# First graph layer of a four-part network: scores issued three pairs ahead with four exp buffers, adjacency transposes through one PSUM bank

## What is computed

```python
y = jnp.linalg.norm(x, axis=-1, keepdims=True)
A = x @ x.T / (y @ y.T) * b
A = jnp.tanh(A / 8.0) * 8.0
A = jnp.exp(A) * A_shape                      # A_shape is the adjacency matrix
A = A / jnp.sum(A, axis=-1, keepdims=True)
x = A @ x
return x @ W.T + bias
```

## Time and profile before

| | |
|---|---|
| median of 3 runs | 1024.88 us (1022.98 to 1025.22) |
| profiled execution, its own time | 1025.94 us |
| its span | 1024.3 us |
| mean granted TensorE clock | 0.842 |
| TensorE matmuls busy in the span | 719.9 us (70%) |
| VectorE | 666.3 us (65%) |
| ScalarE | 451.5 us (44%) |
| first part: first scores / last row sums start | 17.05 us / 159.74 us |

### The profile page before, as it was taken

One profiled execution on the slowest core, in us unless ns is written; L12 is line 12 of the kernel. 1 busy time (PEld: TensorE's weight loads), 2 busy tenths in 40 slices (PEclk: granted clock), 3 DMA queues, 4 the chain that ended last, 5 costly groups with the idle time before them and its releaser, 6 DMA issues.

```text
span 1024.3 us, 14187 instructions
## 1 busy us (share of the span) xinstructions
PE 719.9 (70%) x4705; PEld 529.0 (52%) x4705; DVE 666.3 (65%) x2073; ACT 451.5 (44%) x612; POOL 208.5 (20%) x476
## 2 busy tenths in 40 slices
PE   3999996715999205689999987326855955676274
PEld 2455454314988203358877856115635743666144
DVE  6555656501333227787766516999999999995958
ACT  3877771002333002443445338538656855811041
POOL 3400000274221475000000002213134134310000
PEclk9999996756999656889999999658778877888678
DMA  9176000123777210000000000000000000201001
GB/s 187 29 121 204 1 1 1 52 77 96 218 214 206 71 52 20 1 1 1 2 2 1 2 1 2 0 0 2 1 1 2 2 1 1 83 1 28 0 1 42
DMA packets 49704, 44.12 MB, mean 43 GB/s; under 512 B 7136, under 2 KB 46432, under 8 KB 49120
## 3 DMA queue, kind: packets, MB, share of 16 engines
q1 hardware_dynamic: 37600, 26.47, 8.8%
q0 software_dynamic: 12032, 16.78, 8.0%
HBM read 40.09 MB, written 11.53 MB: 50 GB/s over the span
## 4 chain that ended last, share of the span: by engine, by line
DVE 32%; PE 23%; ACT 3%; issue 3%; DVEq 1%; SPq 0%; DMA 0%; ACTq 0%
PE bank L1763 6%; PE bank L1709 6%; PE bank L1722 4%; DVE big L1296 4%; DVE cand L1227 3%; DVE rm L1128 3%; PE bank L1746 3%; DVE hacc L1222 3%; DVE big L1287 2%; DVE big L1284 2%; DVE cand L1245 2%; DVE top L1240 1%; ACT big L1577 1%; ACT big L1550 1%; PE bank L1903 1%
## 5 line engine op out<-in xcount | busy, mean ns | idle before, releaser
L1577 ACT ACTIVATE big<-bank 128x512 f32<-128x512 f32 x128 | 70.4, 595 | 94.3 <-PE bank L1746 94.0
L1709 PE MATMUL bank<-kk,qq 64*128 64x512 f32 x256 | 82.7, 775 | 32.7 <-ACT big L1550 32.7
L1746 PE MATMUL bank<-ident,big 128*128 128x128 f32 x512 | 80.7, 306 | 34.7 <-DVEq L1319 27.6
L1746 PEld LDWEIGHTS bank<-ident,big 128*128 128x128 f32 x512 | 62.3, 155 | 61.0 <-DVEq L1319 28.3
L714 DVE TENSOR_TENSOR big<-big,bank 128x512 f32<-128x512 f32 x32 | 22.0, 688 | 109.1 <-ACT big L756 109.1
L1550 ACT ACTIVATE big<-bank,negm 128x2048 f32<-128x2048 f32 x32 | 62.7, 1960 | 68.6 <-DVE fsc L1323 50.9
L1296 DVE SCALAR_TENSOR_TENSOR big<-big,st 128x2048 f32<-128x2048 f32 x32 | 73.9, 2348 | 14.3 <-PE bank L1746 14.3
L1026 POOL TENSOR_SCALAR bt<-bt 128x1 f32<-128x1 f32 x16 | 3.1, 195 | 364.1 <-ACT big L1567 224.6
L308 DVE TENSOR_TENSOR big<-big,adjT 128x1024 f32<-128x1024 f32 x32 | 40.0, 1251 | 54.9 <-ACT big L362 54.8
L411 PE MATMUL bank<-xnT 128*128 128x512 f32 x128 | 64.1, 624 | 4.5 <-ACT xnT L339 4.0
L829 PE MATMUL bank<-big 128*128 128x256 f32 x256 | 64.1, 395 | 1.0 <-DMA big<-in_L_ffn_w_dram 0.3
(11 more groups left out here) (325 smaller groups left out, 1556.8 us busy)
## 6 DMA issues: line engine op xcount, KB each, us to landing
big<-in_L_ffn_w_dram SPq DMA_DIRECT2D x96, 128.0 KB
big<-in_adj_dram POOLq DMA_DIRECT2D x8, 512.0 KB, 10.1
xs_scratch<-hacc SPq DMA_DIRECT2D x4, 1024.0 KB, 7.0
big<-xs_scratch POOLq DMA_DIRECT2D x32, 128.0 KB, 3.1
ys_scratch<-big SPq DMA_DIRECT2D x32, 128.0 KB, 2.8
kk<-in_adj_dram POOLq DMA_DIRECT2D x4, 512.0 KB, 12.2
qq<-in_adj_dram POOLq DMA_DIRECT2D x4, 512.0 KB, 12.8
res<-in_x_dram SPq DMA_DIRECT2D x4, 256.0 KB, 5.9
```

Source lines behind the costliest of these rows:

```text
L1577: nc.scalar.activation(MT[:, 4 * q:4 * q + 4, s * P:(s + 1) * P], bank[:, 5 + q % 2, :].rearrange("p (j i) -> p j i", j=4), ACT.Copy).then ...
L1709: nc.tensor.matmul(bank[:, c, :], qq[lo:lo + DA, (g * G + s) * P:(g * G + s + 1) * P], kk[lo:lo + DA, c * CH:(c + 1) * CH], start=True, st ...
L1746: mm = nc.tensor.transpose(bank[:, 5 + q % 2, j * P:(j + 1) * P], mk[:, s, jt * P:(jt + 1) * P], ident[:, :])
```

## The change

- The exp output `e2` has EB = 4 buffers in place of two, and exp(q) waits for multiply(q-4) in place of multiply(q-2).
- TensorE issues the scores AHEAD = 3 pairs ahead. In step q of the loop it issues scores(q+3), transposes(q+2), gather(q); it was transposes(q+2), scores(q+2), gather(q). The first scores and turns before the loop are reordered to match.
- All adjacency transposes go through bank 6, so transposes(q) wait for the copy of q-1 in place of q-2.
- ScalarE copies the transposes of q+1 after exp(q), in place of those of q+2. In the start it takes chunk 2's and 3's turned rows, and the normalised tiles, one pair earlier.
- Two waits go that kept bank 7 free for the row sums.

```diff
+        EB = 4
+        AHEAD = 3
...
-            4 * CH * TPC // 2, 2 * PR, 2 * PR, 4 * PR, PR, CH, D, D)
+            4 * CH * TPC // 2, 2 * PR, EB * PR, 4 * PR, PR, CH, D, D)
...
-                    nc.scalar.activation(pair_of(q % NP, q // NP), two(bankb[:, 6 + q % 2, :]), ACT.Copy
+                    nc.scalar.activation(pair_of(q % NP, q // NP), two(bankb[:, 6, :]), ACT.Copy
...
-                    if q >= 2:
-                        act.wait_ge(pm_ready, q - 1)
-                    nc.scalar.activation(e2[:, q % 2, :], e1[:, q % 2, :], ACT.Exp, scale=8.0).then_inc(exp_done, 1)
-                    if q == 0:
-                        take_adjT(1)
-                    if q in (1, 2):
-                        take_wnT(q + 1)
-                    if q in (1, 2, 3):
-                        xn_of(range(q * TPC, (q + 1) * TPC), 2)
-                    if q + 2 < NQ:
-                        take_adjT(q + 2)
+                    if q >= EB:
+                        act.wait_ge(pm_ready, q - EB + 1)
+                    nc.scalar.activation(e2[:, q % EB, :], e1[:, q % 2, :], ACT.Exp, scale=8.0).then_inc(exp_done, 1)
+                    if q in (0, 1):
+                        take_wnT(q + 2)
+                    if q in (0, 1, 2):
+                        xn_of(range((q + 1) * TPC, (q + 2) * TPC), 2)
+                    if q + 1 < NQ:
+                        take_adjT(q + 1)
...
-                    if q >= 2:
-                        pe.wait_ge(tr_out, q - 1)
+                    if q:
+                        pe.wait_ge(tr_out, q)
...
-                            mm = nc.tensor.transpose(bankb[:, 6 + q % 2, (k * TPC + s) * P:(k * TPC + s + 1) * P],
+                            mm = nc.tensor.transpose(bankb[:, 6, (k * TPC + s) * P:(k * TPC + s + 1) * P],
...
-                    pe.wait_ge(tr_out, min((c + 1) * NP + 2, NQ))
...
                 score(0)
+                score(1)
                 turn_adj(1)
-                score(1)
+                turn_wn(1)
+                score(2)
+                turn_wn(2)
                 for q in range(NQ):
                     c, p = divmod(q, NP)
-                    if q < NC - 1:
-                        turn_wn(q + 1)
-                    if q == NC - 1:
+                    if q == 0:
+                        turn_wn(3)
+                    if q == 3:
...
-                    if c and p == 1:
-                        pe.wait_ge(sum_read, c)
+                    if q + AHEAD < NQ:
+                        score(q + AHEAD)
                     if q + 2 < NQ:
                         turn_adj(q + 2)
-                        score(q + 2)
                     gather(q)
```

More of the change, by code:

```diff
@@ L163, in build @@
         e1 = e1.rearrange("p (s n) -> p s n", s=2)
-        e2 = e2.rearrange("p (s n) -> p s n", s=2)
+        e2 = e2.rearrange("p (s n) -> p s n", s=EB)
         pm = pm.rearrange("p (s n) -> p s n", s=4)
@@ L307, in _ @@
                         dve.wait_ge(acc_done, (q - 3) // NP * (NP - 1) + max((q - 3) % NP, 0))
-                    nc.vector.tensor_tensor(two(pm[:, q % 4, :]), two(e2[:, q % 2, :]), pair_of(p, c), ALU.mult
+                    nc.vector.tensor_tensor(two(pm[:, q % 4, :]), two(e2[:, q % EB, :]), pair_of(p, c), ALU.mult
                                             ).then_inc(pm_ready, 1)
```

## The result

| | before | after |
|---|---|---|
| median | 1023.93 us (1022.81 to 1025.22, 4 runs) | 1046.89 us (1045.03 to 1047.86, 4 runs) |
| profiled execution, its own time | 1025.94 us | 1046.38 us |
| its span | 1024.3 us | 1044.7 us |
| mean granted TensorE clock | 0.842 | 0.845 |
| first row sums / last row sums / next part starts | 63.18 / 159.74 / 165.69 us | 74.91 / 183.10 / 188.73 us |

The change costs 22.96 us. The ratio is 1.0225, with a 95% interval of 1.0208 to 1.0242.

The account below looks back on a forecast made before the run. TensorE's own work was taken to bound the first layer's middle. Start 3.3, steady part 15.2, chunk ends 1.9 and end 3.0 summed to 23.4 us more, giving 1048.3 us, range 1042 to 1057.

Parts of the forecast that it names:

- the closed round: First layer, each pair: scores(q+2), transposes(q+1), ScalarE's copy(q+1), tanh(q+1), scores(q+3) wait in a loop, 4.63 us against 3.94.
- The middle is bound by TensorE, and only 3.1 us could come back: First layer, 22 to 160 us: TensorE busy 134.88 of 138 us, so better overlap could return at most 3.1 us.
- The round of 4.63 us: One pair's loop: scores 1.82, transposes to copy 0.65, copy to tanh 0.92, tanh to next scores 1.24; bounds 4.5 to 4.75.
- Steady part and chunk ends, +15.2 and +1.9: Scores(9) to scores(31): 22 periods longer by 4.63 - 3.94 us give +15.2; three chunk ends at 0.63 us give +1.9.
- Start, +3.3: Layer's start: reordered turns and ScalarE's tiles delay the first pairs, scores(9) at 59.1 us against 55.75.
- End, +3.0: Layer's end: from the start of scores(31) to the last row sums 12.4 us, against 9.4 before.
- Exp buffers, bank, waits of bank 7, adjacency loads: nothing: First layer: four exp buffers, one transposes' bank, the dropped bank 7 waits and later adjacency loads cost or gain nothing.
- The delay goes through whole: After the layer: a barrier stands behind it, so all 23.4 us of delay reach the total time.
- the signs that I had named: Layer's profile: period 4.6 us, scores waiting 0.5 us each (12 to 18 total), ScalarE 1.6, scores(9) near 59, clock 1.00.
- the clock's: Rival, chance 0.06: gaps drop TensorE's clock in the layer; 1073 us with a quarter of the pairs, 1147 with all.
- The rival of a shorter round (4.3 us): Rival, chance 0.03: in the steady part shorter hand-overs and scores of 1.72 us make a turn 4.3 us, total 1038 us.
- The rival "not slower": Rival, chance 0.02: tanh(q+1) ends before scores(q+3) are due, TensorE never waits, up to 3.1 us come back: 1022 us.

Follow-up runs that it names:

- b_bank_exp4: The kernel before with one bank for the adjacency transposes in place of two and four exp buffers, old orders kept: 1024.64 us.
- a_two_banks: The changed kernel with the adjacency transposes back in banks 6 and 7 by turns, with their two waits: 1047.83 us.
- a_extra: The changed kernel with one more ScalarE operation per pair ahead of tanh, a copy of the identity into an unread tile: 1053.69 us.

## Why the prediction was right

The forecast was 1048.3 us, 23.4 over before; measured are 1046.89, 22.96 over before (whose median is 1023.93 now, 0.95 below the one that I had added to). The mechanism, the closed round, was right. That the sum came out within 0.5 us of the measured difference is in part luck: the start was 1.4 us too short and the steady part with its chunk ends 1.4 us too long, and the two cancel. Step by step:

- **The middle is bound by TensorE, and only 3.1 us could come back.** Held: no kernel here has a chunk under 34.16 us.
- **The round of 4.63 us.** Right in kind, and a little too long: it is 4.55 us. The term that was mis-sized is tanh's start to the scores it releases, 1.24 taken from the earlier trace rows, 1.16 measured in the steady part. The earlier trace rows show the scores of pair 5, which wait for a second semaphore as well (see the last section). The others (1.82, 0.65, 0.92) came out as taken.
- **Steady part and chunk ends, +15.2 and +1.9.** Scores(9) to scores(31) took 170.73 - 60.42 = 110.3 us against 94.6: +15.7 for a forecast of +17.1. The last scores and the last row sums:

```profile
170.73 1.98 PE L411 MATMUL bank<-xnT 128*128 128x512 f32 x4 [0.35 <-ACT big L359]
...
183.10 1.95 PE L436 MATMUL bank<-ones,big 128*128 128x1 f32 x16 [0.48 <-DVE big L277]
```

  Sixteen of the 22 rounds lie outside the chunk ends; at 0.08 us less each they explain 1.3 of the missing 1.4 us. Two pairs at a chunk's end cost 39.80 - 6 x 4.55 = 12.5 us, 3.4 over two rounds; I had 3.3.
- **Start, +3.3.** It was +4.7: scores(9) at 60.42 us against 55.75. Missing in my sum was a slow TensorE, in two places. First, scores(0) and scores(1) together took 5.9 us (16.97 to 22.91) where I had 5.35, because the slow pace lasted into scores(1); everything up to scores(3) is 0.5 us late by it. The doubled durations show this pace (3.78 us against 1.94 for scores(0)), but the granted clock is listed as 1.00 for that stretch, so that it was the clock is inferred. Second, TensorE stood 2.87 us before scores(3), and the granted clock fell to 1.2 GHz from 32.1 to 35.5 us. Scores(3) and the transposes behind them took 1.4 us longer, of which ScalarE's tiles hid a part: scores(4) came 1.1 us later behind scores(3) than by my working. I had the gap in my working and counted what follows it at full clock. Shorter rounds up to scores(9) gave back some 0.3 us.
- **End, +3.0.** 183.10 - 170.73 = 12.4 us, as taken, against 9.4.
- **Exp buffers, bank, waits of bank 7, adjacency loads: nothing.** Shown by b_bank_exp4 and a_two_banks. In the changed kernel no exp waits for a multiply and no transposes of the adjacency for a copy or a load, from 17 to 190 us.
- **The delay goes through whole.** The next part starts 23.04 us later (188.73 against 165.69), where my sum had 23.4 (the projection behind the last row sums is 0.3 us shorter than before). In the two profiled executions the spans differ by 20.4 us only. The experts' part had a short stretch at full clock there that the execution before had not: the 32 matmuls of its gate took 5.25 us instead of 7.01, first before, then after:

```profile
174.32 7.01 PE L772 MATMUL bank<-big,xnT 128*128 128x16 f32 x32 [0.72 <-DVE xnT L539]
```

```profile
197.37 5.25 PE L773 MATMUL bank<-big,xnT 128*128 128x16 f32 x32 [0.87 <-DVE xnT L540]
```

This is 1.8 of the 2.6 us by which the spans fall short; the rest was not looked for. The medians are 22.96 us apart and don't show such a gain, and one profiled execution of each kernel can't say how often it occurs.

Of the signs that I had named, the waits of the scores are there (26, 15.7 us in total, within 12 to 18), though with 0.35 us each and not 0.5, and so are ScalarE's waits (1.43 us each for 1.6) and scores(31) near 171 us. Scores(9) are later than the 59 us named, and the clock was not 1.00 throughout.

Of the rivals, the clock's came true in one place and not as a state of the layer. Two windows of the kernel after, the granted clock again the first of the last three numbers:

```profile
32.00:35.40 3.40, 3.40 (x13) 1.71 (x12) 1.22 (x1) 2.40 (x7) 0.00 (x0) 0.51 0.00 0
36.00:180.00 144.00, 130.35 (x540) 62.22 (x538) 73.00 (x84) 95.04 (x97) 13.43 (x12) 1.00 0.27 59
```

With a gap of 0.35 us in each round of 4.55 us, and three gaps of 1.69 us at the chunk ends, TensorE kept 2.4 GHz throughout; after the one gap of 2.87 us it had 1.2 GHz for 3.4 us. The length of a gap alone does not decide it: in a_extra the clock fell after the gap of 1.89 us at the first chunk's end and did not after the same gap at the other two (1.00 from 116 to 122 us and from 157 to 164 us). The Trainium skill's "TensorE: Matmul & The Clock Gate", section "A second HAM failure mode: psum-queue depth-cycling", has short idling between groups of matmuls as a cause of a swinging clock. By that rule, at the rival's price, the kernel would have gone to 1073 us or beyond; these gaps did not do it. The rival of a shorter round (4.3 us) has the sign of my error right, but four times its size: the round was 0.08 us shorter than mine, not 0.33. The rival "not slower" (tanh over before scores are due) is refuted by every steady round: the scores wait 0.35 us for tanh.

## What to carry to other kernels

Issuing work further ahead does not by itself decouple engines that run in order. Write down, for one period, which instruction each wait stands behind on its own engine, and add up every closed round. The period is the longest of these sums per pair, and the busiest engine's work is only one of them. A wait that costs nothing (28.1 us of ScalarE for transposes) starts to cost when an instruction that another engine needs is put behind it, and swapping two statements on one engine, or moving one copy on the other, opens the round again. Where the middle is bound by one engine's work, a greater distance can win only at the ends, and has to be weighed against what it does to the start.

## What was not expected of the hardware

- The hand-over from tanh to scores becomes 0.09 us shorter after pair 7. In the changed kernel the scores of pairs 3 to 7 wait on two semaphores (`s_free` for the tanh, `wnT_out` for the turned rows), and from pair 8 on they wait on the tanh alone. Tanh's start to scores' start is 1.25 or 1.26 us for pairs 3 to 7 (50.10 to 51.36 for pair 7), 1.17 for pair 8 (54.71 to 55.88), and 1.16 after. That the second wait costs the 0.09 us is argued and not shown: it was not tried by itself.

```profile
50.10 1.11 ACT L359 ACTIVATE big<-bank,bs 128x1024 f32<-128x1024 f32 x1
...
51.36 1.95 PE L411 MATMUL bank<-xnT 128*128 128x512 f32 x4 [0.44 <-ACT big L359]
...
54.71 1.11 ACT L359 ACTIVATE big<-bank,bs 128x1024 f32<-128x1024 f32 x1
...
55.88 1.98 PE L411 MATMUL bank<-xnT 128*128 128x512 f32 x4 [0.35 <-ACT big L359]
```

- A ScalarE copy of 128 x 128 with a listed 0.30 us takes a slot of 0.20 us between others. The normalised tiles of the same shape, with a scale and a bias from tiles, take 0.39 us each (1.54 for four).
